# Experts' weights in five places, gathers and norms spread over later units, keys and queries two slots sooner

## What is computed

```python
# layer 0: attention of x over the context, with padding masks, then a layer norm
# layer 1:
x = _layernorm(x + _attn(x, x, x, ..., causal=True), ln1_g, ln1_b)
x = _layernorm(x + _attn(x, encoder_output, encoder_output, ..., False), ln2_g, ln2_b)
x = _layernorm(x + _moe(x, router_w, router_b, e_w1, e_b1, e_w2, e_b2), ln3_g, ln3_b)
# _moe: 8 experts of 128 -> 512 -> 128, each token by its best 2
router_weights = jax.nn.softmax(xf @ rw + rb, axis=-1)
topw, topi = jax.lax.top_k(router_weights, K)
topw = jax.nn.softmax(topw, axis=-1)
combine = jnp.zeros((T, E), xf.dtype).at[jnp.arange(T)[:, None], topi].add(topw)
h = jax.nn.gelu(jnp.einsum('td,edf->etf', xf, w1) + b1[:, None, :], approximate=False)
eo = jnp.einsum('etf,efd->etd', h, w2) + b2[:, None, :]
out = jnp.einsum('etd,te->td', eo, combine)
# layer 2: attention with operands rounded to 8 bits, over x and then over the context,
#          and a feed-forward x = a * gelu(g) @ ff_w2 + ff_b2 + x
# layer 3: 16 query heads of 64 on 4 key heads with rope, then a gated feed-forward
```

## Time and profile before

| | |
|---|---|
| runs | 1717.7, 1697.43 and 1705.72 us, median 1705.72 us |
| profiled execution | 1707.79 us, of which 1706.0 us are the span shown |
| TensorE busy | 1189.4 us (70%), its weight loads 679.7 us |
| VectorE busy | 1101.3 us (65%) |
| ScalarE busy | 902.0 us (53%) |
| GpSimd busy | 676.9 us (40%) |
| instructions | 27685 |
| moved by DMA | 115.53 MB, a mean of 68 GB/s |

### The profile page before, as it was taken

One profiled execution on the slowest core, in us unless ns is written; L12 is line 12 of the kernel. 1 busy time (PEld: TensorE's weight loads), 2 busy tenths in 40 slices (PEclk: granted clock), 3 DMA queues, 4 the chain that ended last, 5 costly groups with the idle time before them and its releaser, 6 DMA issues.

```text
span 1706.0 us, 27685 instructions
## 1 busy us (share of the span) xinstructions
PE 1189.4 (70%) x8785; PEld 679.7 (40%) x8832; DVE 1101.3 (65%) x3127; ACT 902.0 (53%) x2546; POOL 676.9 (40%) x1048
## 2 busy tenths in 40 slices
PE   2688889999967777778233545444436877888888
PEld 1344445555533335767011211112223543554445
DVE  2465676776555664545688999988875557676633
ACT  1343445445534434543566788798884244454542
POOL 5111100010111132442778788887774135443420
PEclk9899999999989989988555555555557979999999
DMA  5221424321153201130644566675562012111000
GB/s 164 56 43 35 76 49 97 68 56 31 30 103 87 44 21 49 44 84 20 164 98 95 106 124 118 114 128 106 103 106 47 15 30 62 28 38 33 14 1 25
DMA packets 263828, 115.53 MB, mean 68 GB/s; under 512 B 215931, under 2 KB 252675, under 8 KB 261507
## 3 DMA queue, kind: packets, MB, share of 16 engines
q1 hardware_dynamic: 258720, 107.34, 31.0%
q0 software_dynamic: 2048, 4.20, 0.8%
q10 hardware_dynamic: 2912, 2.22, 0.4%
HBM read 38.54 MB, written 16.45 MB: 32 GB/s over the span
## 4 chain that ended last, share of the span: by engine, by line
PE 38%; POOL 17%; DVE 17%; issue 15%; ACT 9%; DMA 2%; SPq 1%; DVEq 0%; another core or an unknown queue 0%; POOLq 0%; ACTq 0%
POOL arena L2179 10%; ACT arena L1479 4%; PE acc L1093 4%; DVE minus_top L1870 3%; PE misc L930 3%; PE trans L1070 2%; POOL inv_total L2168 2%; PE trans L1066 2%; PE score L1032 2%; PE misc L936 2%; PE trans L1218 2%; PE score L1131 2%; PE acc L1091 2%; PE score L1230 2%; PE score L1232 1%
## 5 line engine op out<-in xcount | busy, mean ns | idle before, releaser
L2179 POOL TENSOR_SCALAR arena<-arena,inv_total 128x512 f16<-128x512 f32 (+1 forms) x512 | 300.8, 588 | 56.0 <-DVE inv_total L1946 16.5
L1870 DVE TENSOR_REDUCE minus_top<-score 128x4 f32<-128x616 f32 (+4 forms) x256 | 197.2, 806 | 180.4 <-PE score L1036 71.0
L2042 POOL TENSOR_TENSOR rstd<-spread,minus_half 128x4 f32<-128x4 f32 x36 | 37.0, 1028 | 533.1 <-DVE spread L1560 463.8
L1479 ACT ACTIVATE arena<-score,minus_top,exp_scale 128x512 f32<-128x512 f32 (+1 forms) x340 | 210.4, 625 | 24.2 <-POOL arena L2179 13.0
L1426 ACT ACTIVATE arena<-trans 128x512 f32<-128x512 f32 x240 | 141.2, 597 | 146.8 <-PE trans L1070 143.6
L1175 PE MATMUL score<-arena 32*128 32x512 bf16 (+1 forms) x340 | 68.9, 457 | 153.3 <-ACT arena L1479 152.1
L1517 ACT ACTIVATE arena<-arena,minus_top 128x154 f32<-128x154 f32 x256 | 105.1, 412 | 132.6 <-DVE minus_top L2011 132.4
L1952 DVE TENSOR_REDUCE top_score<-score 128x2 f32<-128x1024 f32 (+1 forms) x128 | 135.7, 1060 | 0.5 <-PE score L1175 0.5
L2199 POOL TENSOR_TENSOR arena<-arena,inv_total 128x512 f32<-128x512 f32 x64 | 66.5, 1040 | 147.4 <-DVE inv_total L2019 133.5
L1070 PE MATMUL trans<-arena 128*128 128x512 bf16 (+2 forms) x383 | 123.3, 331 | 2.0 <-issue 0.9
L1032 PE MATMUL score<-arena 128*128 128x154 bf16 x512 | 71.9, 251 | 57.2 <-issue 49.0
(11 more groups left out here) (283 smaller groups left out, 3083.2 us busy)
## 6 DMA issues: line engine op xcount, KB each, us to landing
arena<-q_terms SPq DMA_DIRECT2D x176, 64.0 KB
late<-arena SPq DMA_DIRECT2D x128, 64.0 KB, 2.0
q_terms<-arena SPq DMA_DIRECT2D x36, 128.0 KB
late<-k_terms SPq DMA_DIRECT2D x64, 64.0 KB
arena<-arena SPq DMA_TRANSPOSE x192, 3.1
by_expert<-zeros SPq DMA_DIRECT2D x2, 1472.0 KB, 16.8
arena<-by_expert SPq DMA_DIRECT2D x10, 256.0 KB, 4.2
from_expert<-arena SPq DMA_DIRECT2D x10, 256.0 KB
```

Source lines behind the costliest of these rows:

```text
L1479: ins = nc.scalar.activation(probs[:, i % 3, j, of], quant_score[i % 3][:, j, of], ACT.Exp, bias=minus_top[:, at_col:at_col + 1], scale=ex ...
L1870: nc.vector.tensor_reduce(dst, src, axis=AX.X, op=ALU.max, negate=True).then_inc(top_ready, 1)
L2179: ins = nc.gpsimd.tensor_scalar(codes[:, (i - 1) % CODE_SOURCES, j, to], probs[:, (i - 1) % 3, j, of], inv_total[:, at_col:at_col + 1], HA ...
```

## The change

1. In the cross units from unit 1 on, `K` and `Q` of the next unit move from slots f + 2 and f + 3 to f and f + 1. So that the features are there, `ctx` and `x` of unit u + 2 are made in unit u, at f + 10 and f + 11. As `K` of the next unit then comes ahead of `V` of the present one, the context's tail `ctxT_tail4` has two places.
2. SyncE's order per exact unit becomes: keys out, queries out, keys' reads, queries' reads (unit 4, whose keys come early, keeps its own order).
3. `e_now` has 5 places, and weights are copied 4 blocks ahead, not 2. `staged` has 2 places of one chunk, not 23 blocks; each chunk's load waits for the transposes of the chunk two before, and loads and stores alternate on SyncE.
4. The last scatters of unit 13 stand earlier. `g` is one DMA, not two. Unit 12's gathers stay in a row, those of unit 13 stand in pairs between unit 12's norm steps, and those of units 14 and 15 one to every third step of units 16 and 17; the norms of 14 and 15 follow in units 17 and 18. `M4a` of unit 12 stands one block earlier.
5. `count_norms()` derives the order of the norms, which was a formula, from the tables. The number of compute instructions stays.

```diff
 PAIR_TILES = 2 * TILES
 EXPERT_BLOCKS = 2 * PAIR_TILES + EXPERTS - 1
+EXPERT_PLACES = 5
 CHUNK = 4
...
         f, per, nxt = FIRST_SLOT[u], PER[u], u + 1
         if is_cross(u):
             at(exact, f + 2, ("V", u))
-            if u + 1 < B:
+            if u == 0:
                 at(exact, f, ("ctx", nxt))
                 at(exact, f + 1, ("x", nxt), ("pads", nxt))
+            elif u + 1 < B:
+                at(exact, f, ("pads", nxt))
+            if u + 2 < B:
+                at(exact, f + 10, ("ctx", u + 2))
+                at(exact, f + 11, ("x", u + 2))
             if u:
...
                 if nxt == SELF * B - 1:
                     at(exact, f + 9, ("K", nxt + 1))
                 if nxt != SELF * B:
-                    at(exact, f + 2, ("K", nxt))
-                at(exact, f + 3, ("Q", nxt))
+                    at(exact, f + (0 if u else 2), ("K", nxt))
+                at(exact, f + (1 if u else 3), ("Q", nxt))
...
     f = FIRST_SLOT[11]
     for n in range(TILES):
         at(exact, f + 1, ("S", 12, n))
-    for n in range(TILES):
-        at(exact, f + (2 if n < 2 else 13), ("S", 13, n))
+        at(exact, f + (2 if n < 3 else 11), ("S", 13, n))
     half = EXPERT_BLOCKS
     items = [(0, "N1", 11), (1, "r", 11, 0), (1, "r", 11, 1), (1, "r", 11, 2), (1, "r", 11, 3), (2, "C", 12), (2, "N2", 11),
              (3, "W", 11), (4, "B", 12), (5, "M", 11), (7, "H", 11), (8, "R1", 15), (9, "R2", 15), (10, "R3", 15), (11, "G", 15)]
     items += [(12, "S", u, n) for u in (14, 15) for n in range(TILES)]
     items += [(13, "C", 13), (14, "B", 13), (15, "zv", 13)]
-    for u, slot in ((12, half + 1), (13, half + 2)):
-        items += [(slot, "g", u, n) for n in range(TILES)]
-    for u, slot in ((12, half + 7), (13, half + 14)):
-        items += [(slot, "M4a", u), (slot + 1, "M4b", u), (slot + 2, "M5a", u), (slot + 3, "M5b", u), (slot + 5, "H", u),
-                  (slot + 2, "C", u + 2), (slot + 4, "B", u + 2)]
-    items += [(half + 13, "Q", 16), (half + 16, "K", 16), (half + 20, "V", 16)]
+    items += [(half + 1, "g", 12, n) for n in range(2 * TILES)]
+    items += [(half + slot, "g", 13, n) for n, slot in enumerate((7, 7, 9, 9, 11, 11, 12, 12))]
+    items += [(half + 6, "M4a", 12), (half + 8, "M4b", 12), (half + 9, "C", 14), (half + 10, "M5a", 12), (half + 11, "M5b", 12),
+              (half + 12, "B", 14), (half + 13, "H", 12), (half + 14, "Q", 16), (half + 15, "M4a", 13), (half + 16, "M4b", 13),
+              (half + 16, "C", 15), (half + 17, "K", 16), (half + 18, "M5a", 13), (half + 18, "B", 15), (half + 19, "M5b", 13),
+              (half + 20, "V", 16), (half + 21, "H", 13)]
     for slot, *item in items:
         at(moe, slot, tuple(item))
     for u in QUANT_UNITS:
         f, per = QUANT_BASE[u], QUANT_BASE[u + 1] - QUANT_BASE[u]
         if u == 16:
-            for n in range(TILES):
-                at(quant, f + n, ("g", 14, n))
-                at(quant, f + 12 + 4 * n, ("g", 15, n))
-            for v, first in ((14, f + 8), (15, QUANT_BASE[17])):
+            for v in (14, 15):
+                first = QUANT_BASE[v + 2]
+                for n in range(2 * TILES):
+                    at(quant, first + 5 + 3 * n, ("g", v, n))
                 for slot, name in ((0, "M4a"), (2, "M4b"), (4, "M5a"), (6, "M5b"), (8, "H")):
-                    at(quant, first + slot, (name, v))
+                    at(quant, QUANT_BASE[v + 3] + slot, (name, v))
...
-        e_now, staged = put([P, 3, 2 * FF + CH]), put([P, EXPERT_BLOCKS, D])
+        e_now, staged = put([P, EXPERT_PLACES, 2 * FF + CH]), put([P, 2, CHUNK, D])
...
                     keys = (k_half_ctx if is_cross(u) else k_half)[:, u % 2, :, :, :]
-                    for side, terms, done, stacked in (("k", K_TERMS, k_out, k_stacked), ("q", Q_TERMS, q_out, q_stacked)):
-                        wide = width if side == "k" else TOKENS
-                        terms_of = (k_terms_ctx if side == "k" and is_cross(u) else scratch[side]).ap()
+                    k_terms_of = (k_terms_ctx if is_cross(u) else scratch["k"]).ap()
+                    def read_keys():
+                        sp.wait_ge(k_out, 48 * (u + 1))
+                        if u >= 2 and u != SELF * B:
+                            sp.wait_ge(scoresT_ready, FIRST_SLOT[u - 1])
+                        for s in range(2):
+                            for n, term in enumerate(K_TERMS):
+                                r = slice(s * STACK + n * HD, s * STACK + (n + 1) * HD)
+                                sp.dma_start(keys[r, s, :, :], k_terms_of[s * HD:(s + 1) * HD, term, :, :])\
+                                    .then_inc(k_stacked, 16)
+                    def read_queries(pairs, stacked):
+                        for s in range(2):
+                            for n, term in enumerate(Q_TERMS):
+                                r = slice(s * STACK + n * HD, s * STACK + (n + 1) * HD)
+                                sp.dma_start(q_stack[r, u % 2, pairs, :], scratch["q"].ap()[s * HD:(s + 1) * HD, term, pairs, :])\
+                                    .then_inc(stacked, 16)
+                    for side in "kq":
+                        wide, terms_of = (width, k_terms_of) if side == "k" else (TOKENS, scratch["q"].ap())
+                        terms, done, stacked = (K_TERMS, k_out, k_stacked) if side == "k" else (Q_TERMS, q_out, q_stacked)
                         sp.wait_ge(parts_ready, 2 * u + (1 if side == "k" else 2))
                         if u:
                             sp.wait_ge(stacked, 16 * 2 * len(terms) * u)
                         for t in range(3):
-                            sp.dma_start(terms_of[:, t, :, :].rearrange("r c k -> c r k"), parts[side][:, t, 0:wide])                                .then_inc(done, 16)
...
+                            read_keys()
+                    if u and u != SELF * B:
+                        read_keys()
+                    sp.wait_ge(q_out, 48 * (u + 1))
+                    if u >= 2:
+                        sp.wait_ge(scoresT_ready, FIRST_SLOT[u - 1])
+                    if u == 0:
+                        read_queries(slice(0, 2), q_first)
+                    read_queries(slice(0 if u else 2, PAIRS), q_stacked)
                     if u == 0:
...
-                def load_rows(g):
+                def load_rows(c):
+                    g, k = divmod(c, CHUNKS)
+                    of = slice(k * CHUNK, min((k + 1) * CHUNK, EXPERT_BLOCKS))
                     sp.wait_ge(scattered, 16 * 2 * PAIR_TILES * (g + 1))
-                    for k in range(CHUNKS):
-                        of = slice(k * CHUNK, min((k + 1) * CHUNK, EXPERT_BLOCKS))
-                        if g:
-                            sp.wait_ge(chunk_raised, k + 1)
-                        sp.dma_start(staged[:, of, :], by_expert[g].ap().rearrange("(n p) d -> p n d", p=P)[:, of, :])\
-                            .then_inc(staged_in[k], 16)
+                    if c >= 2:
+                        sp.wait_ge(chunk_raised, c - 1)
+                    sp.dma_start(staged[:, c % 2, 0:of.stop - of.start, :],
+                                 by_expert[g].ap().rearrange("(n p) d -> p n d", p=P)[:, of, :]).then_inc(staged_in[c % 2], 16)
...
-                load_rows(0)
-                for c in range(CHUNKS - 1):
+                for c in range(4):
+                    load_rows(c)
+                for c in range(2):
                     store_rows(c)
-                load_rows(1)
-                for c in range(CHUNKS - 1, 2 * CHUNKS):
+                    load_rows(c + 4)
+                store_rows(2)
+                store_rows(3)
+                for c in range(2):
+                    load_rows(CHUNKS + c)
+                for c in range(4, 2 * CHUNKS):
                     store_rows(c)
+                    if c + 4 < 2 * CHUNKS:
+                        load_rows(c + 4)
...
                 def copy_expert(i):
                     g, n = divmod(i, EXPERT_BLOCKS)
-                    if i >= 3:
-                        dve.wait_ge(down_raised, i - 2)
+                    if i >= EXPERT_PLACES:
+                        dve.wait_ge(down_raised, i - EXPERT_PLACES + 1)
...
-                copy_expert(0)
-                copy_expert(1)
+                for i in range(EXPERT_PLACES - 1):
+                    copy_expert(i)
                 for i in range(ALL_BLOCKS):
-                    if i + 2 < ALL_BLOCKS:
-                        copy_expert(i + 2)
+                    if i + EXPERT_PLACES - 1 < ALL_BLOCKS:
+                        copy_expert(i + EXPERT_PLACES - 1)
...
-                        for k in range(2):
-                            at_no = k * PAIR_TILES + b % 2 * TILES + n
-                            nc.gpsimd.indirect_dma_start(
-                                expert_rows[:, u % 2, k, n, :], None, from_expert[b // 2].ap(),
```

(6 more changed lines are left out.)

66 lines of the change are left out of this document (31 added, 35 removed).

## The result

The changed kernel takes 1642.9 us (median of 4 runs, 1640.09 to 1645.65) against 1707.76 us of the kernel before (median of 4, 1697.43 to 1717.7): a ratio of 0.9621, interval 0.9559 to 0.9683. The forecast was 1653 in a range of 1632 to 1681. The span of the profiled execution is 1638.3 us, 67.7 less than before; the sum on record had 53.4. The gain is of the forecast kind in every part but one, and three of its terms were off.

What follows compares the result with a forecast made beforehand. No engine was busy throughout: time lay in waits, with a different engine or queue ending last per stage. Terms −23.3 − 4.5 − 1.5 − 4.3 − 7.7 − 15.4 + 3.3 = −53.4 gave 1653 us, range 1632 to 1681.

Steps and rivals of the forecast that it cites:

- Exact units, term of 23.3 + 4.5 + 1.5: Exact attention: 23.3 us from smaller stalls at slot 15, 4.5 from clock behind them, 1.5 from unit 2's features moved.
- of clock behind the stalls: Exact units 2, 10 and 11: TensorE's lowered clock after each stall, 1.5 us each, 4.5 in all, bounds 0 and 7.9.
- Self attention at nothing: Self-attention units: SyncE's new order costed at nothing, given a cover of 4 us.
- Start of the experts, 4.3: Experts' start: unit 13's last scatter two slots sooner, so TensorE begins about 651.3 instead of 655.62; gain 4.3, bounds 3 and 5.4.
- To group 1, 7.7: Experts up to group 1: first half 38 for 43.5, chain 28.3 instead of 30.4; 66.3 for 74.0, gain 7.7.
- Second half, 15.4: Experts' second half, counted along gathers and norms: 65.1 us for 80.53, gain 15.4, bounds 2.7 and 26.7.
- Quantised units, −3.3: Units 16 to 18: 16 gathers at 1.7 plus two norms at 5.3, 37.8 against 34.5; loss 3.3, bounds 0 and 8.
- B: Rival: exact units' stacks come hardly sooner, VectorE or ScalarE decides, reads queue; 8.4 instead of 29.3, so 1673; chance 0.12.
- C: Rival: GpSimd's chain in the experts' stage stays; gain there 12.5 instead of 27.4, so 1667; chance 0.12.
- D: Rival: TensorE bounds the experts, chains fit under its work; 8.6 and 11.3 less, 1632; chance 0.04.
- F: Rival: exact and experts' gains lost elsewhere, stall returning as waits for softmax maxima; 1694, no measurable change; chance 0.09.
- E: Rival: slower, TensorE's clock stays at its lower level through the experts' stage; 1739, deciding from granted 0.59; chance 0.03.

Runs made afterwards that it cites:

- the seven kernels: Changed kernel and six follow-up kernels with its same exact stage; start of span to experts' first transposes took 613.5 to 624.1 us, mean 618.8.
- the run with idle work: Changed kernel with idle TensorE matmuls ahead of first scores of units 1, 9, 11 and of chunk 6: 1645.02 us, ratio 0.9656.
- The dense run: Changed kernel with gathers of units 14 and 15 in steps 5 to 12 of units 16 and 17, not every third: 1655.66 us, 0.9689.

## Why the prediction was right, and where it was off

**Exact units, term of 23.3 + 4.5 + 1.5.** The mechanism held: keys' and queries' chain ends last, and both its edits shorten it. For unit 9 the query parts came 4.0 us sooner (16.9 after unit 8's first score instead of 20.9; the forecast's two slots were 4.3) and the stacks 1.7 sooner after the parts (forecast 2.2): 5.7 for the 6.5 of the sum. What failed is the rule "each stall shrinks by the lesser of itself and that" (the shift), because a stall of 0.40 us ahead of unit 3 was taken for no stall. That unit was as much bound by its stacks as the others; TensorE merely used its slow clock up to their arrival. With the clock held up the wait is 2.64 us, and with the change the interval falls from 47.46 to 42.45, by 5.0 where the sum had 3.0. Such an interval is the longer of two: the chain (47.5 us) or TensorE's own time. The second fell as well, from 47.56 − 2.64 = 44.9 with the old slots and the clock up to 42.5 with the new ones (42.45 to 42.48 in all ten kernels that have them), as six transposes left it and TensorE waits 1.5 us around the projections instead of 2.5. So half of the 5.0 is the stacks' earlier arrival and half TensorE's own time, of which the sum had only the transposes.

The 4.5 us "of clock behind the stalls" were priced in the wrong place. In unit 2 the lower clock cost nothing by itself. But TensorE also walks the slots that lead to the next projections, so that a lower clock delays the chain: in unit 10 the first 6 us are at a granted 0.50 in the kernel before and at 1.00 in the changed one and in the run with the slots undone.

```profile
550.59:556.59 6.00, 6.00 (x34) 4.13 (x34) 4.42 (x12) 0.83 (x2) 0.00 (x0) 0.50 0.00 0
```

```profile
541.35:547.35 6.00, 5.54 (x41) 3.01 (x40) 4.92 (x17) 2.03 (x5) 2.58 (x6) 1.00 0.00 0
```

The first is the kernel before, the second the run with the slots undone. The parts for unit 11 are ready 23.7 us after unit 10's first score in the one and 21.1 in the other, with the same slots, and 15.9 in the changed kernel. Unit 10's interval fell by 9.7 where the sum had 8.0. Unit 3's own interval gained 1.8 that I had at zero; TensorE's waits around the projections, for VectorE and ScalarE, fell from 0.71 + 1.36 to 0.87, and they are 1.2 of it. Units 8 to 10 gained 21.1 for 17.9; by the seven kernels' mean it is 21.2.

**Self attention at nothing**: 240.49 to 240.42, right.

**Start of the experts, 4.3** (5.8 with the clock term of unit 11): 5.3 measured in unit 11's interval, but 50.3 to 56.8 us over the seven kernels, mean 53.4: 2.3 on average. The load's wait did go; the rest isn't resolved.

**To group 1, 7.7**: 4.3. The chain's 28.3 was 28.9. The first half was mis-sized: 38 taken, 40.8 measured. I had let five places remove 5.5 of its 8.2 us of loss; they remove 0.7 at most (41.49 with three, inside the width of the kernels with five), and the rest of what was gained came with the wait that is gone ahead of it (granted clock 1.00 for 0.93). The places pay in the eleven blocks behind instead, where without them TensorE comes after the scatters (32.04). The 2.1 us that I gave to the loads' order belong to the places, as far as the runs show: the old order of loads costs nothing. The new wait ahead of group 1 was called at 8.6 and is 10.09, and 4.8 to 7.6 in the other kernels with the same chain.

**Second half, 15.4**: 14.5. The steps on record and as measured, from TensorE's start: first gather 6.4 and 5.65, sums of unit 12 21.3 and 19.97, sums of unit 13 48.1 and 46.82, end 65.1 and 66.00. That the new wait's lower clock would not matter was implied by bounding this half by GpSimd, and the run with idle work shows it.

**Quantised units, −3.3**: +7.0, the one wrong sign, by 10.3 us. Of the 29.2 extra us of unit 16, 23.9 were divided evenly over 14 gathers, 1.7 each, and that price was carried over to lone gathers. A lone one adds 1.25 us to a step of 1.98. Over units 16 and 17 the 16 gathers cost 17 us (79.67 + 86.36 less two units of 71.9 and a norm of 5.3), not 27.2; the norm's price of 5.3 held (77.22 with one, 71.9 without). In the old places two of the pairs carried a pause of 3 us each, and in the new ones they also lie over waits of about 4 us a unit that are paid anyway. The dense run takes back 5.7 of it, the old places 6.9. The bound of 0 on record, "spread gathers fill GpSimd's waits", still lay short of the truth, as it allowed for no gain.

**Rivals.** B falls: for unit 9 the stacks came 5.7 us sooner, and the queries' reads take as long from start to first score right behind the keys' reads (18.7, and 16.3 for unit 11) as 4.2 us after the last of them was issued (18.6 and 16.2). The Trainium skill ("DMA: Bandwidth & Descriptors", on why a DMA increments its semaphore by 16) lets copies of eight rows use eight engines, the lowest-numbered; the DMA share of 0.50 agrees, but that two sets share them costs nothing visible here. Over the last 7 us ahead of unit 9's first score the share is 1.03 in both kernels, as the experts' weights are being loaded, and what that load costs the reads no run here shows. C falls with the second half at 66.00. D is partly true of the first half only. F fell: the 41 us gained up to the experts' stage did not come back as other waits. E did not come near: the clock in the second half is 0.88, above the 0.59 at which it would decide.

**Right for partly offsetting reasons.** The median lies 10 us under the forecast, about what the quantised term missed; the exact units' excess and the experts' shortfall offset each other. The profiled execution lies further off (67.7 for 53.4), as it is at the short end of the exact stage's width (614.61 where the mean is 618.8) and of the stretch behind unit 18 (639.4, mean 645.1).

## What to carry to other kernels

A small wait doesn't mean a small bound: ask whether the engine ahead of it ran at its full pace, since a slowed engine fills a wait without making it shorter, and price the interval as the longer of the chain and the work. A lower clock behind a stall costs nothing where the next wait swallows it, and costs time where the slowed work is itself the bound or leads to the next link of the chain. Take the price of an operation from where it stands alone, not as an average over a crowded stretch; and spread short queue work over steps whose slack is wasted anyway. Before crediting an edit with some microseconds, look at a stretch that it doesn't touch.

## What the runs showed of the hardware

**The same instructions at two paces.** Behind unit 18 nothing differs between the kernels, and yet it takes 637.7 to 654.8 us. Four windows of 32 us, 475 us behind unit 18, of the two executions at the ends of that range, the run with three places and the run with unit 13's gathers in a row:

```profile
1479.17:1511.17 32.00, 25.39 (x146) 12.10 (x142) 22.34 (x109) 18.03 (x71) 12.96 (x17) 1.00 0.17 42
1511.17:1543.17 32.00, 27.37 (x192) 16.80 (x193) 18.09 (x94) 18.88 (x77) 17.14 (x22) 1.00 0.08 20
1543.17:1575.17 32.00, 26.88 (x190) 14.75 (x191) 20.11 (x118) 20.55 (x82) 13.23 (x19) 1.00 0.00 1
1575.17:1607.17 32.00, 28.01 (x144) 16.46 (x144) 10.07 (x36) 9.30 (x20) 3.72 (x5) 1.00 0.00 1
```

```profile
1483.93:1515.93 32.00, 28.17 (x130) 13.24 (x128) 18.08 (x88) 15.99 (x62) 12.29 (x16) 0.79 0.14 36
1515.93:1547.93 32.00, 26.43 (x181) 15.48 (x180) 19.76 (x101) 18.73 (x78) 16.48 (x22) 1.00 0.11 26
1547.93:1579.93 32.00, 27.76 (x149) 14.36 (x148) 15.43 (x88) 16.27 (x65) 10.52 (x15) 0.79 0.00 1
1579.93:1611.93 32.00, 27.24 (x117) 12.93 (x117) 9.55 (x48) 13.15 (x42) 6.80 (x10) 0.73 0.00 1
```

The granted clock is 1.00 throughout in the one and 0.79, 0.79 and 0.73 in the other, with TensorE busy 25 to 28 of 32 us in both. Over the whole stretch the granted clock is 0.80 in the one and 0.77 in the other, and TensorE's busy time is 439.4 and 458.4 us: 19 us more busy time for 17 us more length. In the fourteen executions length and clock go together, so that the clock sets what the same instructions take, by 1% of the kernel's time. What decides it in an execution, no run here shows.

**A pause in close order.** Indirect DMAs on GpSimd follow each other every 1.25 us, but about every seventh or eighth starts 1.9 to 3.6 us late; among the gathers it is the eighth, the sixteenth and so on. It is enough that it stands close to the one just ahead of it: in the kernel before the gathers of unit 15 stand in pairs 11 to 14 us apart, and the eighth still starts 2.94 us late. 3.2 us behind the seventh start it is 2.03 us late (the run with eight steps in a row), and where they are 7.5 us apart or more, none is.
